# FFN weights split to fp16 halves in SBUF and turned by DMA, and an own attention order for block 0

## The chip, the cores and the metric

The kernel runs as one program on one core of one Trainium2 chip. The metric is the device time of one execution in microseconds. The engines of the core work side by side: TensorE (PE, the matrix engine, whose weight loads are shown apart as PEld), VectorE (DVE), ScalarE (ACT), GpSimd (POOL), and SyncE (SP), which here issues most of the DMA transfers. Each runs its own queue of instructions in order and waits for the others through semaphores. Data lie in HBM, in SBUF (128 partitions) and in PSUM (eight banks of 128 x 512 fp32 values), where matmuls write.

## The reference

There are 16 x 256 token ids below 128, so 4,096 positions that share 128 embedding rows. It computes, cut to what matters:

```
h = rms_norm(rms_norm(emb[x], norm_weight) @ proj.T)             # a table of 128 rows serves
q, k, v = layernorm(h) @ Wq.T, @ Wk.T, @ Wv.T                     # 16 heads of 32
q, k = layernorm(q * gamma + beta) / sqrt(32), layernorm(k * gamma + beta)
attn = where(tril, (q @ k.T) ** 2, 0)                             # per head, sequences of 256
h = h + (attn @ v / (attn.sum(-1) + eps)) @ Wo.T
x = fwht(layernorm(h) * SU_ug) / 64                               # Walsh-Hadamard over 512
a = silu(x @ W_gate.T * s_g) * (x @ W_up.T * s_u)                 # 2,048 wide
y = fwht(a * SU_dp) / 64                                          # Hadamard over 2,048
out = h + y @ W_down.T * s_d
```

## The kernel before

Every fp32 operand of a large product is kept as two fp16 halves, a high and a low (the low is what the high leaves of the value), and a product is three fp16 matmuls: high by high, high by low, low by high (`split_mm`, L1067 to L1069). The 4,096 positions are eight blocks of 512 (`NB`), two sequences each. Attention works on the table of 128 rows: `att` holds the squared scores of each pair of table rows, and for a block a matmul with one-hot ids picks columns of it (`picked`, L1204 and L1205), DVE multiplies them by causal counts (`prod<-bank,cnt`, L654, "product" below), ACT takes the high half and POOL the low half (L338) into `p16`. After four heads come the sums with `val` (`SUMS_AT`), the split of the head output `o16` (low half by POOL, L359), its flip on PE (eight 128x128 turns against a unit matrix, L1229, `O_FLIP_AT`) and ACT's copy to `oT`. Then, for each of four row tiles: output matmuls (`WO_AT`), a gathered table row added (`h_row<-h_table,ids_c`, L367, `ROWS_AT`), layer norm and the small Hadamard butterflies on DVE (L697 to L709, L428, L429), halves `x16` (L681), a flip (L1239) and a mix by a fp16 Hadamard matrix (L1247, L1248) into `xT`.

The program is made of slots, 32 to a block. In a slot the FFN of block b and the attention of block b+1 stand one behind the other on each engine (`feed(b, s)`, `attend(b + 1, s)`). Slots 0 to 15 hold one FFN tile each: gate half, up half (each 12 matmuls of 512 columns), ACT's silu gate `sg`, DVE's product `a<-bank,kap,sg` (L723), ACT's high half of `hid` and POOL's low half (L378). Slots 16 to 31 hold the down product, four row tiles, each finished on DVE (L731) and stored by SP (L287). Blocks 1 to 6 run in a loop. Block 0 stands apart: first the loads and the small matrices (table, Wq, Wk, Wv), then 32 slots of attention alone, then its FFN with attention of block 1 beside it.

The FFN's weights are made ready in block 0. Up and gate hold 32 units (128 columns by 512) and down 16. A unit of the first kind is turned on PE in fp32 against a diagonal of its row scales (`turn_unit`, L1062; the diagonals are made by DVE, `group_diag`, L451) into a PSUM bank; ACT copies the high half (L835, `unit`), DVE subtracts for the low (L457). Units 0 to 15 stand in the attention of block 0 (slots 2 to 17), the rest beside its FFN. The scales come from squares on ACT (`gu_square`), a power on POOL (`pair_power`, L316) and a rounding on DVE (`pair_scale`). A down unit is first mixed over rows by DVE (`down_mix`, two fp32 operations of 128x1024, L471 and L472), turned (`down_turn`), copied back by ACT, multiplied by the Hadamard matrix in fp32 (`down_hada`, L1110), and split from that bank by ACT (high) and DVE (low, L479). The order of everything is written out by hand: tuples of slot numbers and the order of the calls in each engine's section; there is no scheduler.

```
UNITS_IN_SLOT = (0, 0) + (1,) * BEFORE + (0,) * 14
DOWN_ORDER = (3, 2, 0, 1)
MIX_BESIDE = (1, 2, 3, 4, 5, 6, 7, 8, 9, 10, 11, 12, 12, 13)
SUMS_AT = (4, 8, 12, 15)
O_FLIP_AT = (5, 9, 13, 17)
ROWS_AT = (17, 19, 21, 23)
WO_AT = (18, 20, 22, 24)
X_FLIP_AT = (21, 23, 25, 27)
X_MIX_AT = (23, 25, 27, 29)
```

Of the kernel before, what the change touches and what calls it, by code (L numbers as in the profile page):

```python
# [52 lines left out]

def down_evicts(p):
    return [p - UNITS_BESIDE - 1] if UNITS_BESIDE < p <= UNITS_BESIDE + 16 else []


def units_beside(p):
    return [BEFORE + p] if p < UNITS_BESIDE else []


def tower(nc, x, emb, norm_w, proj_w, wq, wk, wv, wo, gamma, beta, su_ug, su_dp, wsc_ug, wsc_dp,
# [28 lines left out]
    with ctx:  # L91
# [9 lines left out]
        wgu = sb("wgu", [P, GROUPS, DC, 2, 512], F16)  # L101
# [15 lines left out]
        oT = sb("oT", [P, 2, QUADS, T], F16)  # L117
# [30 lines left out]
        k_o, k_d, s_w = gl[:, 0:1], gl[:, 1:2], gl[:, 10:12]  # L148

# [5 lines left out]
        GU = [words(wgu[:, n, :, :, :].rearrange("p a b c -> p (a b c)")) for n in range(GROUPS)]  # L155
# [47 lines left out]
        gu_ss gu_rn gu_pow gu_diag turned w_hi w_lo  # L203
        d_ss d_mix d_diag sc_ready bound_asked bound_sum bound_low bound_pow bound_done
        d_turned d_copied d_hada d_hi d_lo
# [7 lines left out]
        def column(n):  # L213

            return 4 * (n // 2) + FT * (n % 2)

# [9 lines left out]
        def _(sp):  # L226
# [4 lines left out]
            nc.sync.dma_start(late[:, 1536:1792], c_square).then_inc(S["c_land"], 16)  # L231
            nc.sync.dma_start(small_raw[0], quarters(proj_w)).then_inc(S["p_land"], 16)
            nc.sync.dma_start(nw_b, rows(norm_w, D)).then_inc(S["nw_land"], 16)
# [4 lines left out]
            def gu_load(n):  # L238
                w, g = (w_up if n % 2 else w_gate), n // 2
                for i in range(4):  # L240
                    rows_of_tile = w[512 * g + P * i:512 * g + P * i + P, :].rearrange("p (k d) -> p k d", k=DC)
                    nc.sync.dma_start(raw[n][:, :, i, :], rows_of_tile).then_inc(S[f"gu_land{n}"], 16)
# [12 lines left out]
            down_load(3)  # L255
            for n in range(2, GROUPS):
                gu_load(n)
            down_load(2)
# [5 lines left out]
            def load_ids_rows(n):  # L264
                sp.wait_ge(S["c_land"], 16)
                sp.wait_ge(S["onehotT_ready"], n)
                nc.sync.dma_start(ids_b[:, :], x_rows[bass.ds(n, 1), :].broadcast_to([P, T])).then_inc(S["ids_land"], 16)

            def load_ids_columns(n):
                sp.wait_ge(S["c_land"], 16)  # L270
                sp.wait_ge(S["hrow_land"], 64 * n)
                nc.sync.dma_start(ids_c[:, :], x_cols[bass.ds(n, 1), :, :].rearrange("a p c -> (a p) c"))\
                    .then_inc(S["idc_land"], 16)

            def block_io(b, n):

                for m in range(4):
                    if n is not None and m == 2:
                        load_ids_rows(n)
                    if n is not None and m == 3:  # L280
                        load_ids_columns(n)
# [3 lines left out]
                    else:  # L285
                        sp.wait_ge(S["y_last_done"], b + 1)
                    nc.sync.dma_start(out_rows[bass.ds(b, 1), m, :, :].rearrange("a p d -> (a p) d"), o_out[m][:, :])\  # L287
                        .then_inc(S["stored"], 16)
# [3 lines left out]
            with sp.Fori(0, NB - 2) as b:  # L292
                block_io(b, b + 2)
            block_io(NB - 2, None)
            block_io(NB - 1, None)
# [5 lines left out]
        def _(pool):  # L301
# [30 lines left out]
            pool.wait_ge(S["wo_scale"], 2)  # L332
            power(red[:, 3:4], red[:, 2:3]).then_inc(S["wo_scale"], 1)

            def product(n, h):
                if h < H:
                    pool.wait_ge(S["ph_done"], H * n + h + 1)
                    nc.gpsimd.tensor_tensor(p16[:, 1, h % 4, :], prod[:, h % 2, :], p16[:, 0, h % 4, :], ALU.subtract)\  # L338
                        .then_inc(S["pl_done"], 1)

            def first(n):
                return isinstance(n, int) and n == 0
# [11 lines left out]

            def attend(n, s):
                if s in SUMS_AT:
                    q = SUMS_AT.index(s)
# [3 lines left out]
                if s in ROWS_AT and not first(n):  # L361
# [3 lines left out]
                    pool.wait_ge(S["o_flipped"], QUADS * n + QUADS)  # L365
# [4 lines left out]
                if s in WO_AT:  # L370
                    m = WO_AT.index(s)
                    pool.wait_ge(S["ve_done"], 4 * n + m + 1)
                    power(rstd[:, m:m + 1], ve[:, m:m + 1]).then_inc(S["rstd_done"], 1)
# [7 lines left out]
            for s in range(SLOTS):  # L381
                product(0, s)
                attend(0, s)
                if s in NORM_AT:
# [12 lines left out]
            for s in range(SLOTS):  # L397
                feed(0, s)
                product(1, s)
                attend(1, s)  # L400
                if s == NORM_BESIDE:
                    pair_power(3)
# [12 lines left out]
        def _(dve):  # L415
# [22 lines left out]
            def pair_scale(g):  # L438
# [3 lines left out]
                link(nc.vector.tensor_scalar(pair_columns(rn, g), pair_columns(rnp, g), W_TOP, None, ALU.mult))  # L442

            def group_diag(n):
                c = slice(column(n), column(n) + 4)

                if n > 1:
                    dve.wait_ge(S["turned"], 4 * (n - 1))
                elif n == 1:
                    dve.wait_ge(S["t_ready"], 16)  # L450
                nc.vector.tensor_tensor(gu_diags[n], ident.rearrange("p (a b) -> p a b", a=1).broadcast_to([P, 4, P]),  # L451
# [955 lines left out]
```

## Time and profile before

| | us |
|---|---|
| median of 3 runs | 1418.95 (1417.93 to 1419.73) |
| the profiled execution | 1420.2 |
| its span in the profile | 1418.4 |
| before the first product of block 0 | 68.5 |
| block 0's heads, then its output rows | 59.9, then 38.4 |
| block 0's FFN beside block 1's attention | 211.5 |
| each middle block, six of them | 152.05 |
| last block's FFN | 127.8 |

The profile shows one execution. Times are us from the start of the span unless marked ns. In a row of a timeline the first number is the start and the second the duration; brackets at the end tell how long the engine was idle ahead of it and which engine's work ended that wait. In a row of a group, the numbers behind the bar are busy us in all, mean ns of one, and idle time ahead with its releasers. "Lnnn" is the line of the kernel. The ends of matmuls are modelled, so how fast they follow each other is read from their starts.

### The profile page before, as it was taken

To read this page: it belongs to the slowest core of one execution; us is meant where nothing else is said; L and a number is where in the kernel's file an instruction comes from. 1 tells how busy PE (TensorE), PEld (TensorE's weight loads), DVE (VectorE), ACT (ScalarE), POOL (GpSimd) and SP (SyncE) were. 2 spreads that over 40 slices of the span, in tenths; PEclk is the share of its full clock that TensorE was granted. 3 is DMA by queue.
4 is the path that set the end of the run, shared out by engine and by line. 5 is a ranking of instruction groups with operands and counts; after the bars stand their busy time and mean duration, and the time that the engine had idled before them with its cause. 6 is when DMAs were issued, how large, how long until landed. Compare 5 with 4: busy or idle time off the path is not lost.

```text
span 1418.4 us, 20319 instructions
## 1 busy us (share of the span) xinstructions
PE 1334.5 (94%) x7993; PEld 676.7 (48%) x7993; DVE 532.4 (38%) x1049; ACT 458.0 (32%) x767; POOL 423.6 (30%) x371
## 2 busy tenths in 40 slices
PE   5575598999999999999999999999999999999999
PEld 3363255554444444454454444544445444544444
DVE  1655567654322343226222432234223523251110
ACT  4453564441233223332243123412333224312220
POOL 0342143332143313432244213420434124420210
PEclk9887799999999999999999999999999999999999
DMA  8900000000100010001000100001000100010000
GB/s 288 287 14 1 1 0 1 1 0 31 38 1 1 23 39 8 0 9 45 16 1 1 45 24 0 1 31 38 1 1 9 51 9 1 1 46 15 0 1 30
DMA packets 34125, 39.42 MB, mean 28 GB/s; under 512 B 6596, under 2 KB 23288, under 8 KB 33528
## 3 DMA queue, kind: packets, MB, share of 16 engines
q1 hardware_dynamic: 30528, 28.99, 6.3%
q0 software_dynamic: 2560, 8.39, 2.0%
q8 instruction: 72, 1.18, 0.4%
q10 hardware_dynamic: 952, 0.75, 0.2%
q14 instruction: 13, 0.11, 0.0%
HBM read 29.47 MB, written 8.65 MB: 27 GB/s over the span
## 4 chain that ended last, share of the span: by engine, by line
PE 89%; DVE 5%; ACT 3%; issue 1%; POOL 1%; DMA 1%; SPq 0%; DVEq 0%; ACTq 0%
PE bank L1067 25%; PE bank L1068 25%; PE bank L1069 25%; PE bank L1219 3%; PE bank L1062 2%; PE bank L1204 2%; PE bank L1205 2%; PE bank L1229 1%; PE bank L1110 1%; PE bank L1239 1%; DMA hid<-in_L_tok_norm_weight 1%; PE bank L1060 1%; DVE wgu L457 1%; PE bank L1247 0%; PE bank L1248 0%
## 5 line engine op out<-in xcount | busy, mean ns | idle before, releaser
L1067 PE MATMUL bank<-xT,wgu 128*128 128x512 f16 x1024 | 389.0, 380 | 1.4 <-DVE xT L688 1.4
L1069 PE MATMUL bank<-xT,wgu 128*128 128x512 f16 x1024 | 389.1, 380 | 0.0
L1068 PE MATMUL bank<-xT,wgu 128*128 128x512 f16 x1024 | 389.1, 380 | 0.0
L378 POOL TENSOR_TENSOR hid<-a,hid 128x512 f16<-128x512 f32 x128 | 147.9, 1155 | 526.1 <-ACT hid L835 526.1
L723 DVE SCALAR_TENSOR_TENSOR a<-bank,kap,sg 128x512 f32<-128x512 f32 x128 | 96.1, 751 | 486.0 <-PE bank L1069 334.8
L1068 PE MATMUL bank<-wd,hid 128*128 128x512 f16 x512 | 194.0, 379 | 0.0
L1069 PE MATMUL bank<-wd,hid 128*128 128x512 f16 x512 | 194.0, 379 | 0.0
L1067 PE MATMUL bank<-wd,hid 128*128 128x512 f16 x512 | 194.0, 379 | 0.0
L338 POOL TENSOR_TENSOR p<-prod,p 128x512 f16<-128x512 f32 x128 | 153.2, 1199 | 135.8 <-ACT p L835 135.7
L835 ACT ACTIVATE hid<-a 128x512 f16<-128x512 f32 x128 | 80.6, 630 | 278.8 <-DVE a L723 278.8
L1069 PEld LDWEIGHTS bank<-xT,wgu 128*128 128x128 f16 x1024 | 100.3, 98 | 121.5 <-issue 1.1
L1067 PEld LDWEIGHTS bank<-xT,wgu 128*128 128x128 f16 x1024 | 100.4, 98 | 117.0 <-DVE xT L688 2.3
L1068 PEld LDWEIGHTS bank<-xT,wgu 128*128 128x128 f16 x1024 | 100.3, 98 | 114.3 <-issue 0.8
L982 ACT ACTIVATE sg<-bank,sc 128x512 f32<-128x512 f32 x128 | 87.2, 681 | 126.1 <-PE bank L1069 68.6
L835 ACT ACTIVATE p<-prod 128x512 f16<-128x512 f32 x128 | 79.7, 627 | 128.3 <-PE bank L1219 111.7
L835 ACT ACTIVATE sg<-wide,rstd 128x512 f16<-128x512 f32 x32 | 23.1, 722 | 219.7 <-DVE wide L429 219.7
L654 DVE TENSOR_TENSOR prod<-bank,cnt 128x512 f32<-128x512 f32 x128 | 86.6, 681 | 8.7 <-ACT cnt L835 8.0
L312 POOL TENSOR_TENSOR rstd<-ve,mhalf 128x1 f32<-128x1 f32 x32 | 32.3, 1009 | 188.5 <-DVE ve L706 188.5
L1069 PEld LDWEIGHTS bank<-wd,hid 128*128 128x128 f16 x512 | 50.1, 98 | 60.4
L1068 PEld LDWEIGHTS bank<-wd,hid 128*128 128x128 f16 x512 | 50.1, 98 | 58.3 <-issue 0.3
L1067 PEld LDWEIGHTS bank<-wd,hid 128*128 128x128 f16 x512 | 50.1, 98 | 58.1 <-issue 0.2
L697 DVE SCALAR_TENSOR_TENSOR h<-bank,gl,h_row 128x512 f32 (+1 forms) x28 | 21.0, 751 | 98.0 <-PE bank L1069 97.2
(183 smaller groups left out, 1389.5 us busy)
## 6 DMA issues: line engine op xcount, KB each, us to landing
out<-a SPq DMA_DIRECT2D x24, 256.0 KB, 2.1
wgu<-in_L_ffn_W_gate SPq DMA_DIRECT2D x16, 256.0 KB, 5.5
wgu<-in_L_ffn_W_up SPq DMA_DIRECT2D x16, 256.0 KB, 4.8
wd<-in_L_ffn_W_down SPq DMA_DIRECT2D x4, 1024.0 KB, 9.9
ids_b<-in_x SPq DMA_DIRECT2D x8, 256.0 KB, 4.2
out<-h_row SPq DMA_DIRECT2D x8, 256.0 KB, 2.0
xT<-in_L_tok_proj_weight SPq DMA_DIRECT2D x1, 1024.0 KB, 8.5
p<-in_L_attn_Wq SPq DMA_DIRECT2D x1, 1024.0 KB, 14.4
```

The costliest lines, as they stand in the source:

```text
L312: return nc.gpsimd.tensor_tensor(dst, src, mhalf[:, 0:src.shape[1]], ALU.pow)
L338: nc.gpsimd.tensor_tensor(p16[:, 1, h % 4, :], prod[:, h % 2, :], p16[:, 0, h % 4, :], ALU.subtract)\
L378: nc.gpsimd.tensor_tensor(hid[:, 1, s, :], a32[:, :], hid[:, 0, s, :], ALU.subtract)\
L654: nc.vector.tensor_tensor(prod[:, s % 2, :], PICK[s % 2][:, :], cnt[:, :], ALU.mult)\
L723: nc.vector.scalar_tensor_tensor(a32[:, :], bank[:, :], kap[:, s:s + 1], sg[:, :], ALU.mult, ALU.mult).then_inc(S["a_done"], 1)
L835: return nc.scalar.activation(dst, src, ACT.Copy, **kw)
L982: nc.scalar.activation(sg[:, :], bank[:, :], ACT.Silu, scale=sc[:, s:s + 1]).then_inc(S["silu_done"], 1)
L1062: last = mm(bank[:, i * P:(i + 1) * P], pieces(i), rights(i), start=True, stop=True)
L1067: mm(dst, w[0], v[0], start=first, stop=False)
L1068: mm(dst, w[0], v[1], start=False, stop=False)
L1069: return mm(dst, w[1], v[0], start=False, stop=final)
L1219: last = mm(HEADS[m // 2][:, 4 * (m % 2) + j, :], p16[:, p, j, m * P:(m + 1) * P], val[:, w, 4 * q + j, :], start=first, stop=final, skip_ ...
```

## The change

The change does five things.

1. The 32 gate and up units are no longer turned on PE. The raw rows lie in SBUF as loaded; the row scale multiplies them there, and a high and a low half go into `stage`, a ring of three buffers. For units 0 to 7 ACT scales and copies the high half and DVE subtracts the low (`unit_low`, L540); for units 8 to 31 POOL scales in place (`unit_scaled`, L422), ACT copies and POOL subtracts (`unit_low`, L426). SP then issues one DMA transpose for each unit from `stage` into `wgu` (`unit_turn`). Units 0 to 15 stand in slots 2 to 9 and 16 to 23 of block 0's attention, the rest two to a slot beside slots 0 to 7 of its FFN.
2. The 16 down units are mixed by DVE two to a slot in slots 0 to 7 of block 0's FFN, split three to a slot in slots 9 to 14, turned by DMA as well, and then multiplied by the Hadamard matrix as two fp16 matmuls, in the slot behind the split, in two banks by turns. ACT and DVE split the result as before.
3. In blocks 1 to 7 the flips of `o16` and `x16` are DMA transposes that SP issues (`o_turn`, `x_turn`), eight to a block. SP's loop over the blocks is written out. The row gather waits for the first output matmuls (`wo_ready`) instead of the last flip.
4. Block 0's attention keeps its flips on PE, and has an order of its own (the tables whose names end in 0), a second buffer for `p16`, and two banks for the gate in slots 0 to 7 of its FFN.
5. Ahead of it: `norm_w` is loaded before `proj_w`; each group of FFN weights is one load of 1 MB; the counts and small units 12 to 15 come earlier, and the value matmuls, the squares and split of Wo and its units go into the slots.

Of the tables of numbers and the changed functions, cut to the core:

```diff
+RING = 3
+UNIT_AT = tuple(range(2, 10)) + tuple(range(16, 24))
+UNITS_BESIDE = 8
+MIX_BESIDE = (0, 0, 1, 1, 2, 2, 3, 3, 4, 4, 5, 5, 6, 6, 7, 7)
+SPLIT_BESIDE = (9, 9, 9, 10, 10, 10, 11, 11, 11, 12, 12, 12, 13, 13, 13, 14)
...
+HEADS_AT0 = (4, 8, 12, 16)
+O_AT0 = (5, 9, 13, 16)
+O_FLIP_AT0 = (6, 10, 14, 17)
+WO_AT0 = (18, 19, 20, 21)
+X_HIGH_AT0 = (19, 20, 22, 23)
+X_FLIP_AT0 = (21, 22, 23, 24)
...
+        GATE0, UP0, D_HADA = [banks[0], banks[1]] * 4 + [banks[0]] * 8, banks[2], [banks[3], banks[1]]
...
+            def o_turn(n, q):
+                if q == 0:
+                    sp.wait_ge(S["wo_ready"], 4 * n)
+                sp.wait_ge(S["ol_done"], QUADS * n + q + 1)
+                nc.sync.dma_start_transpose(oT[:, q, :, :].rearrange("p l (m t) -> p (l m) t", t=P),
+                                            o16.rearrange("p l d -> p (l d)")).then_inc(S["oT_land"], 16)
+
+            def x_turn(n, m):
+                sp.wait_ge(S["xl_done"], 4 * n + m + 1)
+                sp.wait_ge(S["xhada_ready"], 4 * n + m)
+                nc.sync.dma_start_transpose(xn16.rearrange("p (k t) -> p k t", t=P),
+                                            x16.rearrange("p l d -> p (l d)")).then_inc(S["xn_land"], 16)
...
-                    pool.wait_ge(S["o_flipped"], QUADS * n + QUADS)
+                    pool.wait_ge(S["wo_ready"], 4 * n + 1)
...
+            def unit_scaled(x):
+                pool.wait_ge(S["gu_scaled"], x // 8 + 1)
+                nc.gpsimd.tensor_scalar(unit_raw(x), unit_raw(x), unit_scale(x), None, ALU.mult).then_inc(S["st_scaled"], 1)
+
+            def unit_low(x):
+                pool.wait_ge(S["st_hi"], x + 1)
+                nc.gpsimd.tensor_tensor(stage[x % RING][:, 1, :], unit_raw(x), stage[x % RING][:, 0, :], ALU.subtract)\
+                    .then_inc(S["st_low"], 1)
...
+            def unit_low(x):
+                dve.wait_ge(S["st_hi"], x + 1)
+                nc.vector.scalar_tensor_tensor(stage[x % RING][:, 1, :], unit_raw(x), unit_scale(x), stage[x % RING][:, 0, :],
+                                               ALU.mult, ALU.subtract).then_inc(S["st_lo"], 1)
...
+            def down_hada(v):
+                if v > 1:
+                    pe.wait_ge(S["d_lo"], v - 1)
                 if v == 0:
...
+                pe.wait_ge(*landed(UNITS + v))
+                w = wd[:, DOWN_ORDER[v // 4], v % 4, :, :, :].rearrange("p l f d -> p l (f d)")
+                mm(D_HADA[v % 2][:, :], hada16[:, :], w[:, 0, :], start=True, stop=False)
+                mm(D_HADA[v % 2][:, :], hada16[:, :], w[:, 1, :], start=False, stop=True).then_inc(S["d_hada"], 1)
```

How the order moves at three places. First POOL, in slots 0 to 3 of block 0's FFN. Before (`hid<-a,hid` is the FFN tile's low half, `p<-prod,p` the low half of a head, `h<-h,mhalf` a power for the scales):

```order
L378 TENSOR_TENSOR hid<-a,hid 128x512
L338 TENSOR_TENSOR p<-prod,p 128x512
L378 TENSOR_TENSOR hid<-a,hid 128x512
L338 TENSOR_TENSOR p<-prod,p 128x512
L378 TENSOR_TENSOR hid<-a,hid 128x512
L338 TENSOR_TENSOR p<-prod,p 128x512
L316 TENSOR_TENSOR h<-h,mhalf 128x2x4
L378 TENSOR_TENSOR hid<-a,hid 128x512
```

And after, in slots 1 and 2 (`wgu<-wgu,h` scales a unit in place, `h<-wgu,h` is its low half):

```order
L422 TENSOR_SCALAR wgu<-wgu,h 128x512 x2
L461 TENSOR_TENSOR hid<-a,hid 128x512
L426 TENSOR_TENSOR h<-wgu,h 128x512 x2
L433 TENSOR_TENSOR p<-prod,p 128x512
L422 TENSOR_SCALAR wgu<-wgu,h 128x512 x2
L461 TENSOR_TENSOR hid<-a,hid 128x512
```

Two operations to a slot have become six: the scalings stand ahead of the tile's low half, the low halves of the units ahead of the head's.

Second DVE, in slot 10 (and the first row of slot 11) of block 0's FFN. Before (`wd<-wd` mixes, `wd<-bank3,gl,wd` is the low half of a finished down unit):

```order
L654 TENSOR_TENSOR prod<-bank4,cnt 128x512
L479 SCALAR_TENSOR_TENSOR wd<-bank3,gl,wd 128x512
L723 SCALAR_TENSOR_TENSOR a32<-bank1,kap,sg 128x512
L479 SCALAR_TENSOR_TENSOR wd<-bank3,gl,wd 128x512
L471 TENSOR_TENSOR wd<-wd 128x1024
L472 SCALAR_TENSOR_TENSOR wd<-wd 128x1024
L654 TENSOR_TENSOR prod<-bank5,cnt 128x512
```

And after (`h1<-wd,wsd_s,h1` is the low half of a down unit ahead of its turn, in `stage`):

```order
L735 TENSOR_TENSOR prod<-bank4,cnt 128x512
L834 SCALAR_TENSOR_TENSOR a32<-bank2,kap,sg 128x512
L540 SCALAR_TENSOR_TENSOR h1<-wd,wsd_s,h1 128x512 x3
L558 SCALAR_TENSOR_TENSOR wd<-bank3,gl,wd 128x512
L558 SCALAR_TENSOR_TENSOR wd<-bank1,gl,wd 128x512
L558 SCALAR_TENSOR_TENSOR wd<-bank3,gl,wd 128x512
L735 TENSOR_TENSOR prod<-bank5,cnt 128x512
```

The three low halves of the next units stand ahead of the three that finish the last ones; the mixes are gone from here.

Third SP, for one middle block. Before (a store of a row tile each, and the next ids):

```order
L287 DMA out<-a 128x512
L284 REGISTER_ALU
L287 ISA
L287 DMA out<-a 128x512
L266 REGISTER_ALU
L267 ISA
L267 DMA ids_b<-in_x 128x512
L284 REGISTER_ALU
L287 ISA
L287 DMA out<-a 128x512
L271 REGISTER_ALU
L272 DMA ids_c<-in_x 128x4x1
```

And after:

```order
L327 DMA_TRANSPOSE oT<-h_row 128x8x128 x4
L333 DMA_TRANSPOSE prod<-sg 128x8x128
L352 DMA out<-a 128x512
L333 DMA_TRANSPOSE prod<-sg 128x8x128
L352 DMA out<-a 128x512
L333 DMA_TRANSPOSE prod<-sg 128x8x128
L306 DMA ids_b<-in_x 128x512
L352 DMA out<-a 128x512
L333 DMA_TRANSPOSE prod<-sg 128x8x128
L311 DMA ids_c<-in_x 128x4x1
L352 DMA out<-h_row 128x512
```

The four turns of `o16` (its place in SBUF is named `h_row` here) stand ahead of the block's stores, and the four of `x16` (`prod<-sg`) between them, the fourth behind the third store.

## Rows read from the trace of the kernel before

**Rows 1.** The page, busy time of each engine in us, share, instructions.

```profile
PE 1334.5 (94%) x7993; PEld 676.7 (48%) x7993; DVE 532.4 (38%) x1049; ACT 458.0 (32%) x767; POOL 423.6 (30%) x371
```

**Rows 2.** Windows: length, busy us (instructions) by PE, PEld, DVE, ACT, POOL; PEclk, DMA share, GB/s.

```profile
68.50:128.40 59.90, 36.84 (x381) 30.70 (x381) 31.61 (x74) 32.48 (x63) 26.50 (x23) 0.80 0.06 16
128.40:166.80 38.40, 20.30 (x91) 8.94 (x91) 23.72 (x57) 17.40 (x39) 6.25 (x6) 0.72 0.00 1
166.80:378.30 211.50, 201.79 (x1216) 112.64 (x1217) 123.22 (x200) 85.67 (x154) 61.42 (x47) 0.98 0.03 11
530.40:682.40 152.00, 152.00 (x925) 73.62 (x924) 51.83 (x106) 45.14 (x69) 49.41 (x44) 1.00 0.05 17
```

**Rows 3.** Timeline of PE in a middle block: start, duration, line, operation.

```profile
1087.98 0.61 PE L1229 MATMUL bank<-c,h_row 128*128 128x128 f16 x8
1088.43 0.38 PE L1067 MATMUL bank<-wd,hid 128*128 128x512 f16 x1
1088.64 0.38 PE L1068 MATMUL bank<-wd,hid 128*128 128x512 f16 x1
...
1091.02 0.38 PE L1067 MATMUL bank<-wo_t,oT 128*128 128x512 f16 x1
```

**Rows 4.** Groups of instructions in block 0's FFN, 166.8 to 378.3.

```profile
L378 POOL TENSOR_TENSOR hid<-a,hid 128x512 f16<-128x512 f32 x16 | 18.5, 1157 | 99.8 <-ACT hid L835 99.8
...
L1062 PE MATMUL bank<-h,wgu 128*128 128x128 f32 x128 | 17.9, 284 | 2.5 <-DVE wgu L457 1.7 <-DVE h L451 0.7
L1062 PE MATMUL bank<-h,wd 128*128 128x128 f32 x128 | 17.8, 285 | 1.8 <-DVE h L528 1.8
...
L1110 PE MATMUL bank<-h 128*128 128x512 f32 x32 | 17.4, 626 | 2.1 <-DVE wd L479 2.1
```

**Rows 5.** Timeline of DVE and POOL in block 0's FFN.

```profile
187.05 1.22 DVE L471 TENSOR_TENSOR wd<-wd 128x1024 f32<-128x1024 f32 x1
187.07 2.21 POOL L338 TENSOR_TENSOR p<-prod,p 128x512 f16<-128x512 f32 x1
...
188.30 2.07 DVE L472 SCALAR_TENSOR_TENSOR wd<-wd 128x1024 f32<-128x1024 f32 x1
...
205.45 1.23 DVE L472 SCALAR_TENSOR_TENSOR wd<-wd 128x1024 f32<-128x1024 f32 x1
```

**Rows 6.** Timeline ahead of and in block 0's heads, PE and DVE.

```profile
54.03 3.70 PE L1177 MATMUL bank<-oT,hid 128*128 128x512 f32 x8 [0.69 <-ACT oT L835]
...
56.88 0.16 DVE L615 TENSOR_REDUCE h<-h 128x1 f32<-128x4 f32 x1 [9.33 <-ACT sg L832]
...
76.04 0.69 DVE L654 TENSOR_TENSOR prod<-bank,cnt 128x512 f32<-128x512 f32 x1 [0.68 <-PE bank L1205]
...
85.67 0.69 DVE L654 TENSOR_TENSOR prod<-bank,cnt 128x512 f32<-128x512 f32 x1
...
88.14 0.68 DVE L654 TENSOR_TENSOR prod<-bank,cnt 128x512 f32<-128x512 f32 x1
```

**Rows 7.** Timeline of DVE and PE in block 0's FFN: tile products 0 and 8, first down matmul.

```profile
176.01 0.75 DVE L723 SCALAR_TENSOR_TENSOR a<-bank,kap,sg 128x512 f32<-128x512 f32 x1 [0.65 <-PE bank L1069]
...
245.03 0.75 DVE L723 SCALAR_TENSOR_TENSOR a<-bank,kap,sg 128x512 f32<-128x512 f32 x1 [0.91 <-issue]
...
322.57 0.38 PE L1067 MATMUL bank<-wd,hid 128*128 128x512 f16 x1
```

**Rows 8.** Timeline of POOL, ACT and DVE in the same middle block.

```profile
1085.05 1.15 POOL L359 TENSOR_TENSOR h_row<-wide,h_row 128x512 f16<-128x512 f32 x1 [0.56 <-ACT h_row L835]
...
1128.95 0.59 ACT L835 ACTIVATE xT<-bank 128x512 f16<-128x512 f32 x1
...
1130.18 0.74 DVE L731 SCALAR_TENSOR_TENSOR a<-bank,gl,h 128x512 f32<-128x512 f32 x1
```

**Rows 9.** DMA issues: tiles, queue, kind, count, KB each, median us to landing.

```profile
out<-a SPq DMA_DIRECT2D x24, 256.0 KB, 2.1
...
wgu<-in_L_ffn_W_up SPq DMA_DIRECT2D x16, 256.0 KB, 4.8
```

More of the change, by code:

```diff
@@ L331, in _ @@
             pair_power(0)
[L332 to L342, printed above, removed]
             def first_rows():
@@ L919, in product @@
             def product(n, s):
-                if s == 0:
+                if s == 0 and not first(n):
                     act.wait_ge(S["count_ready"], n + 1)
@@ L926, in product @@
                     act.wait_ge(S["p_done"], i + 1)
-                    if s % 4 == 0:
+                    if s % 4 == 0 and not first(n):
                         act.wait_ge(S["heads_ready"], QUADS * n + s // 4)
-                    copy(p16[:, 0, s % 4, :], prod[:, s % 2, :]).then_inc(S["ph_done"], 1)
+                    if s % 4 == 0 and s >= 8 and first(n):
+                        act.wait_ge(S["heads_ready"], s // 4 - 1)
+                    copy(p_pair(n, s)[:, 0, s % 4, :], prod[:, s % 2, :]).then_inc(S["ph_done"], 1)
@@ new lines, in head_high, with xT_high @@
+            def head_high(n, q):
+                act.wait_ge(S["o_done"], QUADS * n + q + 1)
+                if not first(n) and not (isinstance(n, int) and q == 0):
+                    act.wait_ge(S["oT_land"], 16 * (QUADS * (n - 1) + q))
+                copy(o16[:, 0, :], wide[:, :]).then_inc(S["oh_done"], 1)
+            def xT_high(n, m):
+                act.wait_ge(S["xhada_ready"], 4 * n + m + 1)
+                if m == 0:
+                    act.wait_ge(S["up_ready"], FT * n)
+                copy(xT[:, 0, :, m * P:(m + 1) * P], PICK[1][:, :].rearrange("p (k t) -> p k t", t=P))\
+                    .then_inc(S["xThi_done"], 1)
@@ L931, in attend, with x_high @@
+            def x_high(n, m):
+                act.wait_ge(S["xm_done"], 4 * n + m + 1)
+                act.wait_ge(S["rstd_done"], 4 * n + m + 1)
+                if first(n):
+                    act.wait_ge(S["flip_ready"], m)
+                elif not (isinstance(n, int) and m == 0):
+                    act.wait_ge(S["xn_land"], 16 * (4 * (n - 1) + m))
+                copy(x16[:, 0, :], wide[:, :], scale=rstd[:, m:m + 1]).then_inc(S["xh_done"], 1)
             def attend(n, s):
+                if s - 1 in WO_AT:
+                    x_high(n, WO_AT.index(s - 1))
@@ L1155, in _, with count @@
                 last.then_inc(S["qk_ready"], 1)
+            def count(n, bank):
+                for i in range(2):
+                    c = SEQ * i
+                    mm(bank[:, c:c + SEQ], onehot[:, 2 * i, :], cum0, start=True, stop=False)
+                    last = mm(bank[:, c + P:c + SEQ], onehot[:, 2 * i + 1, :], cum1, start=False, stop=True)
+                last.then_inc(S["count_ready"], 1)
+            pe.wait_ge(S["par_land"], PARAMS)
+            pe.wait_ge(S["onehot_ready"], 2)
+            count(0, COUNT0)
+            pe.wait_ge(S["wv_diag"], 2)
+            for u in range(12, 16):
+                small_unit(u)
             def qk_turn(i):
@@ L1263, in feed_half @@
             def feed_half(s, half, bank, done):
-                n = 2 * (s // 4) + half
-                c = slice(P * (s % 4), P * (s % 4) + P)
+                n, i = 2 * (s // 4) + half, s % 4
                 for k in range(DC):
-                    last = split_mm(bank[:, :], [wgu[:, n, k, l, c] for l in range(2)],
+                    last = split_mm(bank[:, :], [wgu[:, n, i, l, k, :] for l in range(2)],
                                     [xT[:, l, k, :] for l in range(2)], k == 0, k == DC - 1)
@@ L1357, in _ @@
                 attend(1, s)
+                for v in down_third(s, 2):
+                    down_hada(v)
             pe.wait_ge(S["y_done"], 3)
```

747 lines of the change are left out of this document (377 added, 370 removed).

## The prediction

> **What bounds the kernel now.** The page first: TensorE (PE) is busy 94% of the span, the other engines under 40% [rows 1]. So I cut the span where PE changes its work and read the windows [rows 2]. A middle block is PE solid for 152.0 us: 512-column fp16 matmuls start every 0.216 us (1088.43, 1088.64), and a flip of eight turns holds the queue from 1087.98 to 1088.43, 0.45 us [rows 3]. Ahead of block 0's FFN it is otherwise: in the heads (68.5 to 128.4) and the output rows (128.4 to 166.8) PE is busy 57 of 98 us, and a chain over DVE, ACT and POOL sets the pace. Block 0's FFN takes 211.5 us, 59.5 more than a middle block, and holds the fp32 turns and Hadamards: 17.9, 17.8 and 17.4 us in three groups [rows 4]. Those sums count the overlap of neighbouring matmuls, so I take 53 less a fifth, 43 us, for what they hold of the queue.
>
> **The port.** [rows 5] decides much of what follows. POOL's subtraction took 2.21 us at 187.07 where its kind takes 1.16 [rows 4]; beside it ran VectorE's (DVE's) fp32 mix from 187.05 (1.22), and the next mix took 2.07 where an undisturbed one took 1.23 (205.45). The three fit if POOL waits for the first mix and the second mix for POOL: a POOL operation and a DVE operation with two SBUF inputs take turns. The Trainium skill (GPSIMD Engine Reference, the table of SBUF interfaces at its head) says that GpSimd shares SBUF ports with DVE and contends with DVE instructions of two SBUF inputs. By that rule, which this trace bears out, the change is costlier than a count of busy time tells: the old splits read PSUM and SBUF, the new ones read SBUF twice.
>
> **The change, part by part.**
>
> *Before the heads.* DVE waited 9.33 us for the squares behind which Wo's stood, until 56.88 [rows 6]. Those squares, Wv's diagonals and small units 12 to 15 now stand elsewhere, so head 0's product follows the features: they end at 47.6; two turns, a copy and the scores 3.1; a square, two highs and a low 2.5; a pick 0.4. That is 53.6. The norm weight is issued one transfer earlier; I give that 1.5 us, by choice between nothing and the 4.8 of a 256 KB piece [rows 9]. Product 0 at 52 for 68.5. Behind it two picks 0.9, the value matmuls 3.7 (54.03), pick 2 0.4 and handovers 0.8: product 2 at 57.8 where it was at 76.04 [rows 6]: -18.2.
> *Heads.* An old slot with a unit, product to product, took 2.47 us (85.67 to 88.14). A new one: product 0.64, ACT copy 0.6; then ACT's high 0.6 and DVE's low, which reads two SBUF tensors when POOL's product (1.16) has begun: 0.64 + 0.6 + 1.16 + 0.7 = 3.1. Eight slots 25; fit and two head rows 4; slots 10 to 15, without units, 12.5; then POOL's queue ahead of the last heads (pair 1's power, two scalings, two products, the last low, flip and copy) 12.7. That is 54.2 for 52.4 (76.0 to 128.4): +1.8.
> *Output rows.* The new order overlaps the low half of row m-1 with row m; alone I take 36 for 38.4. But POOL now has a scaling and a subtraction in each slot, 2 us beside the five two-input operations of a row's norm, and ACT a split and a square: +2 for each of four rows. 44.2: +5.8. The FFN starts at 156.2, -10.6 in all.
> *Block 0's FFN, slots 0 to 7.* PE needs 24 x 0.216 + 0.43 = 5.6 us a slot. POOL: two scalings, feed, two lows, product = 4 x 1.16 + 2c. The price c of a one-input POOL operation has no row; 1.16 above, half of it below; I take 0.9. DVE: two mixes, four operations of 1.23, all of two inputs, so they take turns with POOL: 6.4 + 4.9 + 1.1, while POOL waits for ACT's split and copy, = 12.4. The next product needs POOL's feed of the last, and PE's next up half needs the product. The first product comes at 9.2 (176.01 - 166.8); three slots go at some 10.2 while the queues fill, four at 12.4, and the slot without units at 9.5: product 8 ends at 99, before at 78.2 (245.03 - 166.8) [rows 7].
> *Slots 9 to 15.* Product 9 at 104. Hadamard 0 stands ahead of the next up half and needs the first turn: split 1.3, low 0.7, turn T + 0.1; with T = 3.3, 5.4 later. From slot 10 on, third 2's Hadamard waits on PE for the low half of third 0 (two banks), and on DVE that low half stands behind three new splits, which wait for ACT. From the end of an up half: product 0.85, ACT copy 0.6, high 0.6, first split 0.6, then DVE 3 x 0.65 and the low half 0.65 = 5.2; PE had work for 0.9. A slot is 5.2 + 0.43 + 2.6 + 0.43 + 2.6 = 11.3, four times, the fifth 9.9, then 5.6 + 0.7. The first down matmul comes 170.8 after the FFN's start; before, 322.57 - 166.8 = 155.8 [rows 7]: +15. PE's own work fell by 43 - 6.9, but is not what ends here.
> *Turns by DMA, blocks 1 to 7.* PE loses eight flips, 3.58 us a block, and ACT eight copies of 1.0. Were PE bound throughout, that is the gain. POOL ends the last low half at 1086.20 [rows 8]; Wo, at 1091.02 [rows 3], would come 0.45 earlier, so T may be 4.4. The row gather waits for Wo instead of the flip, which brings row 0 3.4 us later, but it catches up 1.1 a row. The fourth x turn stands on SP behind the third store: from the mix of slot 27, 0.2 + ACT 0.6 + DVE 0.7 + finish 0.75 [rows 8] + issue 0.45 = 2.7; the mix of slot 29 is 24 x 0.216 = 5.2 away. So T may be 2.5 there. T has no row: a store of the same 256 KB lands in 2.1 us, a weight piece in a full queue in 4.8 [rows 9]. I take 3.3, with a store in front; bounds 2.1 and 4.8. Stall 0.8, so -2.8 a block: six blocks -16.7, block 0's second half -2.2 + 0.8 = -1.4. Were T 2.1, seven blocks gain 5.6 more; at 4.8, 7 x 1.9 + 1.5 = 15 less.
> The Trainium skill has two prices. Advanced Engine Details and Errata, X-Bar Transpose, calls such DMAs as fast as regular ones, which fits the range; VectorE: DVE Perf Modes, The three transpose paths, has 1309 ns for one 128x128 by DMA and 390 ns on TensorE. Eight blocks in a row by that table would be an estimate of 10.5 us and the time over 1500; no run here shows either.
>
> **Sum** against the profiled execution: -10.6 + 15 - 1.4 - 16.7 = -13.7; 1420.2 - 13.7 = 1406.5. The median of the three runs is 1.25 lower, so 1405.
>
> **Rivals.**
> A: POOL and DVE do not hold each other. Slots 0 to 7 then follow POOL alone, 6.4 + 1.1 = 7.5 to 8: product 8 at 67, -32; heads -5, rows -6: 1362. For it: one pair of kinds is all that [rows 5] shows. 0.17.
> B: the three-unit slots do not stall, because ACT and DVE run ahead of PE: -20: 1385. The order of the queues speaks against it. 0.07.
> C, slower: turns land late. From T = 3.3 every us costs 7 (fourth x turn) and 1 (Hadamard 0), above 4.4 another 7 (Wo). 8 x 1.1 = 8.8, then 4.9 / 15 = 0.3: from T = 4.7 on the kernel is slower. At 6 it is 8.8 + 24 + 4 (slots 10 to 13) more: 1442. For it: a turn is 2-byte pieces, and the 256 KB weight piece took 4.8 already; against: SP's queue is empty in these stretches, and 2.1 is what it then takes. 0.22.
> D, no change: the later gather holds the rows 2 us more a block: 7 x 2 = 14, 1419. 0.08, half of it slower.
> My own case, 0.46: 1380 to 1428, by c (0.6 to 1.16: -4, +3), T (-6, +15) and chains of 5 us each way in four stages; of it 0.41 faster, 0.03 same, 0.02 slower.
>
> **Numbers.** No change is within 0.2% (2.8 us), about what a measurement can tell. Faster 0.41 + 0.17 + 0.07 = 0.65, same 0.03 + 0.04 = 0.07, slower 0.02 + 0.22 + 0.04 = 0.28. Leaving out half of C and the last of A, 8 in 10 lie in 1365 to 1440.
>
> **What would show it.** Wo's first matmul near 112, the FFN's first near 156; DVE's a<-bank in slots 3 to 7 some 12 us apart, with mixes and POOL rows above 2 us; in slots 10 to 13 PE waiting for DVE's wd of two units back, 11 us a slot; first down matmul at 327; middle blocks of 149.3, with one gap of 0.8 us at the last matmul that reads prod. It is wrong if the turn DMAs land in over 4.7 us, if mixes stay at 1.23 beside POOL, or if middle blocks take 148.5 or more than 151.

## The result, and the profile after

The changed kernel took 1425.76 us (median of 4 runs, 1425.33 to 1427.61); the kernel before, run again beside it, 1418.44 (1415.86 to 1419.73). The ratio is 1.0056, with a 95% interval of 1.0039 to 1.0074: slower by 7.3 us where I forecast 14 faster. The two profiled executions, which everything below compares, lie 5.1 us apart.

The page of the changed kernel, busy time and PE's granted clock in 40 slices, beside [rows 1]:

```profile
span 1423.5 us, 18640 instructions
...
PE 1280.5 (90%) x7161; PEld 599.2 (42%) x7161; DVE 540.8 (38%) x1030; ACT 406.7 (29%) x711; POOL 497.4 (35%) x419
...
PEclk9656788888999999999999999999999999999999
```

PE was busy 54 us less and the span grew by 5.1. The windows by stage, which answer to [rows 2] (columns as there): the heads until the output rows' first matmul, the output rows, block 0's FFN to tile product 9, from there to its first down matmul, and a middle block:

```profile
52.00:115.40 63.40, 30.73 (x281) 16.90 (x282) 35.49 (x72) 34.24 (x69) 34.30 (x29) 0.61 0.31 73
115.40:156.00 40.60, 20.54 (x91) 8.65 (x92) 24.85 (x50) 17.21 (x35) 22.63 (x18) 0.71 0.28 52
156.00:258.60 102.60, 70.39 (x366) 31.04 (x367) 78.33 (x99) 41.33 (x86) 85.47 (x55) 0.84 0.25 47
258.60:341.80 83.20, 54.88 (x284) 23.13 (x283) 32.52 (x50) 32.24 (x53) 18.43 (x15) 0.85 0.29 54
546.86:696.50 149.64, 149.02 (x861) 69.71 (x860) 51.72 (x106) 37.72 (x61) 49.30 (x44) 1.00 0.13 31
```

| stage | before | forecast | after |
|---|---|---|---|
| head 0's product at | 68.5 | 52 | 52.0 |
| FFN of block 0 starts at | 166.8 | 156.2 | 156.0 |
| from there to product 8 | 78.2 | 99 | 91.2 |
| to product 9 | 88.6 | 104 | 102.7 |
| to the first down matmul | 155.8 | 170.8 | 185.8 |
| first down matmul to next block | 55.7 | 54.3 | 55.4 |
| six middle blocks | 912.3 | 895.6 | 898.5 |
| last FFN | 127.8 | 127.8 | 127.8 |

By stage: -10.8, +30.0, -0.3 and -13.8, together the 5.1 of the spans. Three stages came within 3 us of their terms. One did not: between product 9 and the first down matmul lie 83.2 us, before 67.2, forecast 66.8. Slot 11 of it, from its tile product to the gate half of slot 12, changed kernel, timeline of PE and DVE:

```profile
283.20 0.75 DVE L834 SCALAR_TENSOR_TENSOR a<-bank,kap,sg 128x512 f32<-128x512 f32 x1 [4.68 <-issue]
...
285.83 2.08 DVE L540 SCALAR_TENSOR_TENSOR h<-wd,wsd_s,h 128x512 f16<-128x512 f32 x3 [1.88 <-ACT h L942]
...
287.83 1.40 DVE L558 SCALAR_TENSOR_TENSOR wd<-bank,gl,wd 128x512 f16<-128x512 f32 x2
288.63 0.56 PE L1201 MATMUL bank<-wd,hada 128*128 128x512 f16 x1 [4.66 <-DVE wd L558]
...
289.83 0.64 PE L1186 MATMUL bank<-xT,wgu 128*128 128x512 f16 x1
290.26 0.63 PE L1187 MATMUL bank<-xT,wgu 128*128 128x512 f16 x1
...
292.27 0.38 PE L1186 MATMUL bank<-xT,wgu 128*128 128x512 f16 x1
292.49 0.38 PE L1187 MATMUL bank<-xT,wgu 128*128 128x512 f16 x1
```

The third Hadamard waits 4.66 us for the low half that stands behind three others (L540 x3): the stall as forecast. What I had left out follows it: the matmuls then start 0.43 us apart for three microseconds, the lower of the clock's two levels (1.2 GHz), before they return to 0.22 (2.4 GHz). Between 262 and 340, 56 matmuls start late, most of them 0.43 us behind the last: 10.8 us in all.

The slow matmuls aren't settled by the wait alone. The run "Norm weight late" below has the same code in slots 9 to 15. Slot 14 there and in the changed kernel, first the changed kernel, timeline of PE:

```profile
327.58 0.61 PE L1201 MATMUL bank<-wd,hada 128*128 128x512 f16 x1 [3.33 <-DVE wd L558]
327.98 0.63 PE L1202 MATMUL bank<-wd,hada 128*128 128x512 f16 x1
```

```profile
330.38 0.39 PE L1201 MATMUL bank<-wd,hada 128*128 128x512 f16 x1 [3.33 <-DVE wd L558]
330.61 0.38 PE L1202 MATMUL bank<-wd,hada 128*128 128x512 f16 x1
```

The wait is 3.33 us in both. In the first, 13 matmuls behind it are slow and the slot takes 13.1 us (granted clock 0.74), in the second none is and it takes 10.4 us (1.00). So 2.7 of the 83.2 us were the luck of this execution; in the other the stage took 80.5.

### The profile page after: what moved, and what is told of

The parts are those of the page before. It is cut to its first block and busy times, and to the rows that moved or that the text cites. A ratio compares the mean times of both kernels' runs of the same rounds, so it can differ in the third digit from the quotient of the medians.

```text
span 1423.5 us, 18640 instructions
## 1 busy us (share of the span) xinstructions
PE 1280.5 (90%) x7161; PEld 599.2 (42%) x7161; DVE 540.8 (38%) x1030; ACT 406.7 (29%) x711; POOL 497.4 (35%) x419
## 5 line engine op out<-in xcount | busy, mean ns | idle before, releaser
L1185 PE MATMUL bank<-xT,wgu 128*128 128x512 f16 x1024 | 396.5, 387 | 5.5 <-DVE a L834 4.0
L1186 PE MATMUL bank<-xT,wgu 128*128 128x512 f16 x1024 | 395.7, 386 | 0.0
L1187 PE MATMUL bank<-xT,wgu 128*128 128x512 f16 x1024 | 394.8, 386 | 0.0
L461 POOL TENSOR_TENSOR hid<-a,hid 128x512 f16<-128x512 f32 x128 | 149.7, 1170 | 479.2 <-ACT hid L942 479.2
L433 POOL TENSOR_TENSOR p<-prod,p 128x512 f16<-128x512 f32 x120 | 141.4, 1181 | 121.1 <-ACT p L942 121.1
L1185 PEld LDWEIGHTS bank<-xT,wgu 128*128 128x128 f16 x1024 | 102.1, 100 | 131.4 <-issue 10.5
L1187 PEld LDWEIGHTS bank<-xT,wgu 128*128 128x128 f16 x1024 | 101.7, 99 | 126.0 <-issue 9.1
L942 ACT ACTIVATE hid<-a 128x512 f16<-128x512 f32 x128 | 80.5, 629 | 255.1 <-DVE a L834 255.1
L1186 PEld LDWEIGHTS bank<-xT,wgu 128*128 128x128 f16 x1024 | 101.7, 99 | 122.0 <-issue 8.1
L942 ACT ACTIVATE p<-prod 128x512 f16<-128x512 f32 x120 | 74.2, 624 | 118.9 <-PE bank L1326 107.3
L735 DVE TENSOR_TENSOR prod<-bank,cnt 128x512 f32<-128x512 f32 x128 | 86.5, 680 | 11.4 <-ACT cnt L942 9.4
```

The lines of the kernel that those rows point to most:

```text
L433: nc.gpsimd.tensor_tensor(pair_of_head[:, 1, h % 4, :], prod[:, h % 2, :], pair_of_head[:, 0, h % 4, :], ALU.subtract)\
L461: nc.gpsimd.tensor_tensor(hid[:, 1, s, :], a32[:, :], hid[:, 0, s, :], ALU.subtract)\
L735: nc.vector.tensor_tensor(prod[:, s % 2, :], PICK[s % 2][:, :], cnt[:, :], ALU.mult)\
L942: return nc.scalar.activation(dst, src, ACT.Copy, **kw)
L1185: mm(dst, w[0], v[0], start=first, stop=False)
L1186: mm(dst, w[0], v[1], start=False, stop=False)
```

## The experiments

Where a row says "product 9", it is the tile product's start behind the FFN's start. A time without a number of runs is of one run; the four of the changed kernel lie within 2.3 us, and differences of that size are read from the stages alone.

**Low half first.** DVE's queue in slots 10 to 14:

```
-                feed(0, s, UP0)
+                for v in down_third(s, 0):
+                    down_unit(v)
+                feed(0, s, UP0)
...
-                for v in down_third(s, 0) + down_third(s, 1):
+                for v in down_third(s, 1):
```

> The changed kernel, with DVE's low half of the first finished down unit of a slot put ahead of the tile product, so that the third Hadamard (same bank) need not wait for three new low halves. Theory 1, order of DVE's queue plus slow matmuls behind each wait: slots 10 to 14 took 13.4 us each; with the wait of 4.66 us gone a slot is PE's 6.9 us, or, since the first Hadamard of the next slot then waits for its turn (about 3.2 us after its issue), some 10 to 11 us. Five slots: 12 to 17 us off, time 1409 to 1414. Rival, the latency of the turns sets these slots already: no change, 1424 to 1427. Either way slots 0 to 8 stay as they were (product 8 at 91 us after the FFN's start).

1416.51 us: 9 off, less than the theory's 12 to 17. From product 9 to the first down matmul it took 71.3 us for 83.2. The wait for DVE went, and the one for the turn came (timeline of PE, this kernel):

```profile
278.54 0.38 PE L1203 MATMUL bank<-wd,hada 128*128 128x512 f16 x1 [2.95 <-DMA wd<-h]
...
288.57 0.59 PE L1203 MATMUL bank<-wd,hada 128*128 128x512 f16 x1 [2.96 <-DMA wd<-h]
...
311.48 0.49 PE L1203 MATMUL bank<-wd,hada 128*128 128x512 f16 x1 [2.91 <-DMA wd<-h]
```

Slots took 9.9 to 13.0 us for 13.4. The first and second of these waits are alike, but behind the first no matmul is slow (a slot of 10.0 us) and behind the second 15 are (13.0). Both mechanisms are there, one behind the other: an order that frees DVE's low half uncovers the turn's latency.

**No mixes.** The butterflies of the down weights cut to one column, so the down weights stay unmixed:

```
-                link(nc.vector.tensor_tensor(v[:, :, 1, :], v[:, :, 0, :], v[:, :, 1, :], ALU.subtract))
+                link(nc.vector.tensor_tensor(v[:, :, 1, 0:1], v[:, :, 0, 0:1], v[:, :, 1, 0:1], ALU.subtract))
```

> The changed kernel with DVE's mixes of the down weights cut to a sliver of one column of each piece (the down weights are left unmixed, so this work is left out). Theory 1, POOL and DVE take turns at SBUF: with four DVE operations of two SBUF inputs gone from each of slots 0 to 7, POOL's operations fall back to 1.15 and 1.56 us, a slot to POOL's 7.8 plus about 1 us, and product 8 stands at 75 to 80 us after the FFN's start for 91.2: 11 to 16 us off, time 1410 to 1415. Rival, POOL's own work sets these slots whatever DVE does: product 8 at 88 to 91, time 1423 to 1426. Second rival, DVE's own queue sets them: product 8 below 70, since PE needs only 5.6 us a slot.

1409.28 us, product 8 at 74.6: the theory's case, a little better. POOL's operations in this kernel, and what the same kinds took in the changed one (timeline of POOL, then of POOL and DVE in the changed kernel):

```profile
195.91 1.15 POOL L433 TENSOR_TENSOR p<-prod,p 128x512 f16<-128x512 f32 x1
197.03 3.10 POOL L422 TENSOR_SCALAR wgu<-wgu,h 128x512 f32<-128x512 f32 x2
```

```profile
165.89 4.32 POOL L426 TENSOR_TENSOR h<-wgu,h 128x512 f16<-128x512 f32 x2
...
167.12 2.07 DVE L551 SCALAR_TENSOR_TENSOR wd<-wd 128x1024 f32<-128x1024 f32 x1
169.22 2.06 DVE L550 TENSOR_TENSOR wd<-wd 128x1024 f32<-128x1024 f32 x1
...
170.17 2.13 POOL L433 TENSOR_TENSOR p<-prod,p 128x512 f16<-128x512 f32 x1
```

Beside mixes a subtraction takes 2.1 us and a mix 2.07; apart they take 1.15 and 1.22. It is the pattern of [rows 5]: they take turns. In this kernel all of POOL's low halves in slots 0 to 8 are back at about 1.15 us, and its scalings at 1.56. Its work in a slot is 3.10 + 1.16 + 2.27 + 1.15 = 7.7 us, and a slot took 8.3 in the mean, so it is the likely bound. This run also takes DVE's own 4.9 us of mixes out of each slot, so it does not show how much of the 16.6 us is the port and how much DVE's queue.

**Flips only.** The kernel before with this part of the change alone: `o_turn` and `x_turn` on SP in blocks 1 to 7, its loop written out, PE's flips kept for block 0 (`if first(n) and s in O_FLIP_AT`), the gather behind `wo_ready`. In part:

```
-                    pool.wait_ge(S["o_flipped"], QUADS * n + QUADS)
+                    pool.wait_ge(S["wo_ready"], 4 * n + 1)
...
+            for q in range(QUADS):
+                o_turn(1, q)
+            for b in range(NB):
+                block_io(b)
```

> The kernel before, with one part of the change alone: the flips of the head outputs and rows of blocks 1 to 7 as DMA transposes, and the row gather behind the first output matmuls. Theory 1, this part is worth what the middle blocks of the changed kernel show: six blocks from 152.05 to 149.7 us, and 0.3 to 1.5 us in block 0's FFN: 1403 to 1405. Rival, the gain of the middle blocks needs something else of the change (the split gate banks, a shorter block 0): middle blocks stay above 151 and the time above 1412.

1403.83 us (4 runs, 1402.96 to 1405.31), ratio 0.9903 (0.9881 to 0.9924). This part alone makes the kernel 1% faster. A middle block of it:

```profile
538.00:688.00 150.00, 149.32 (x864) 70.01 (x862) 51.74 (x106) 37.73 (x61) 49.66 (x45) 1.00 0.14 31
```

The six took 900.1 for 912.3, near the 898.5 of the changed kernel. Its profiled execution also began its FFN at 163.5 instead of 166.8, with nothing changed ahead of it but the layout of `oT`: the loads landed earlier (the norm weight was used at 11.71 for 13.04). So some 3 us of the changed kernel's -10.8 are likely the profiled execution of before, not the change. The kernels below that share the changed kernel's code up to there have product 0 at 51.6 to 53.4, so one profile tells such a start only to a microsecond or two.

**ACT and DVE split units 16 to 31.** POOL's `unit_scaled` and `unit_low` are gone beside the FFN; ACT copies with the scale, DVE subtracts:

```
-                for x in units_beside(s):
-                    unit_scaled(x)
                 feed(0, s)
-                for x in units_beside(s):
-                    unit_low(x)
```

> The changed kernel, with units 16 to 31 split as units 0 to 7 are: ACT scales and takes the high half, DVE the low half, and POOL has no part in it (four POOL operations of a slot, 2 x 1.56 + 2 x 1.15 us, replaced by two DVE operations of about 1.1 us and ACT scaling as it copies). Theory 1: DVE is then the busiest, 0.65 + 0.75 + 4 x 1.23 + 2 x 1.13 = 8.6 us a slot and up to 1 us of collisions: product 8 at 75 to 80 us after the FFN's start, time 1410 to 1415. Rival, DVE was the bound already and gets two operations more: product 8 at 95 to 105, time 1430 to 1440.

1416.88 us, 9 off; product 8 at 86.2, between the theory (75 to 80) and the changed kernel's 91.2, product 9 at 92.4 for 102.7. The window to product 9 shows what took over:

```profile
156.20:248.60 92.40, 74.50 (x377) 32.42 (x378) 84.55 (x116) 42.87 (x86) 36.54 (x23) 0.86 0.28 49
```

DVE is busy 84.6 of 92.4 us, and PE waits for its tile product (1.28 and 2.36 us behind products 3 and 4; the matmuls behind the first keep their spacing of 0.22, behind the second they fall to 0.43 after four). My 8.6 us a slot allowed up to 1 us of collisions; slots took 9.2 and more, and 9 of the 32 mixes still took 2.06 us or more.

**Hadamards half a slot later.** The first behind the up half, the second behind the attention, the third behind the next slot's gate half, on PE, ACT and DVE alike. PE's part:

```
                     feed_half(s, 0, GATE0[s], S["gate_ready"])
-                    for v in down_third(s, 0):
+                    for v in down_third(s - 1, 2):
                         down_hada(v)
...
                     feed_half(s, 1, UP0, S["up_ready"])
-                    for v in down_third(s, 1):
+                    for v in down_third(s, 0):
                         down_hada(v)
```

> The changed kernel with the three down Hadamards of a slot moved later by half a slot on PE, ACT and DVE: the first behind the up half, the second behind the attention, the third behind the gate half of the next slot. Each turn then has 5 us and more to land, and each bank a half slot to be emptied. Theory (now in two parts: the wait for DVE's low half with one order, the wait for the turn with the other, and after each wait some 8 matmuls at double spacing): both waits go, slots 10 to 14 take 7 to 8 us for 13.4, and the first down matmul comes 50 to 58 us after product 9 for 83.2: time 1395 to 1402. Rival: DVE and ACT cannot do three splits and three evictions in such a slot (5.9 and 6.1 us by their rows, beside 1.4 and 1.9 of the attention's): slots above 9 us, time above 1405.

1399.05 us, 27 off, by order alone. From product 9 to the first down matmul it took 54.4 us for 83.2, in the range. The window of that stage:

```profile
259.60:314.00 54.40, 44.47 (x285) 19.83 (x284) 32.57 (x50) 31.91 (x53) 18.35 (x15) 1.00 0.48 83
```

The work is that of the fourth window above (285 matmuls, 32.6 us of DVE), the granted clock 1.00 for 0.85. The waits for the low half are shorter, not gone: none is over 2.1 us, where they were 3.3 to 4.7. Slots 10 to 13 took 8.7 to 9.8, more than the 7 to 8 expected; the rival was right that DVE and ACT now set them (PE waits for the low half, and DVE 1.88 us a slot for ACT's high half), and wrong on the time.

**Both.** The last two edits together.

> Both edits together: units 16 to 31 split by ACT and DVE without POOL, and the down Hadamards half a slot later. Theory: the two stages add up; product 9 at 92 us after the FFN's start as without the second edit, then 50 to 58 us: time 1384 to 1392. Rival: the gain of one is lost in the other because both queue on DVE: above 1395.

1388.50 us: 1425.8 - 8.9 - 26.7 = 1390.2 if they only added. They do, within what single runs tell.

**Mixes spread,** on top of both:

```
-MIX_BESIDE = (0, 0, 1, 1, 2, 2, 3, 3, 4, 4, 5, 5, 6, 6, 7, 7)
+MIX_BESIDE = (0, 0, 1, 2, 2, 3, 4, 4, 5, 6, 6, 7, 8, 9, 10, 11)
```

> As the run with both edits, and the mixes spread over slots 0 to 11 (one or two to a slot) instead of two in each of slots 0 to 7. In slots 0 to 7 PE waited 1.3 to 2.4 us a slot for DVE's tile product, which stood behind two mixes. Theory, DVE's queue is the bound of these slots: product 9 comes at 78 to 84 us for 92, slots 9 to 11 grow by at most 1 us each: 6 to 12 us faster than the run with both edits. Rival, something else paces them (the single up bank, ACT): less than 3 us.

1388.14 us: a miss. Product 9 came at 85.7 for 91.6, but product 9 to the first down matmul took 60.2 for 55.2. The mixes moved into slots 8 to 11 lengthened that stage by 5.0 us where the other gained 5.9: DVE's work was moved, and by this it bounds both stages.

**Fourth turn ahead of the third store.**

```
                     if b + 2 < NB and m == 2:
                         load_ids_rows(b + 2)
+                    if b + 1 < NB and m == 2:
+                        x_turn(b + 1, 3)
```

> The changed kernel with the fourth turn of x16 issued by SP ahead of the block's third store instead of behind it. Theory: PE's one gap of 0.87 us in a middle block, at the last mix, is this turn standing behind the store; it shrinks to the spacing of 0.22, so the six middle blocks take 149.0 to 149.2 us each for 149.75, and the time falls by 3 to 5 us to 1421 to 1423. Rival: the turn is late for its latency alone, and the gap stays.

1421.72 us, 4.0 off, as expected. The gap of the changed kernel, and SP's queue there:

```profile
687.25 0.34 SPq L352 DMA_DIRECT2D out<-a  x1
687.68 1.30 SPq L333 DMA_TRANSPOSE prod<-sg  x1
...
690.83 0.39 PE L1357 MATMUL bank<-prod,hada 128*128 128x512 f16 x1 [0.49 <-DMA prod<-sg]
```

In the edited kernel the turn is issued at 684.60 and PE has no idle row there; middle blocks take 148.9 to 149.7, 895.05 for six, 3.4 less.

**All that helped**, the spread mixes, and the second sum over the bound (where PE had stood 5.64 us in slot 2) one slot later on all engines. PE's part of that:

```
-                    if s == BOUND_BESIDE + 1:
+                    if s == BOUND_BESIDE + 2:
                         bound_sum(1)
```

> The edits that helped, together: units 16 to 31 split by ACT and DVE, down Hadamards half a slot later, mixes spread over slots 0 to 11, the fourth turn of x16 ahead of the third store; and one new edit, the second sum over the bound moved one slot later on all engines, because PE stood 5.64 us there (waiting for DVE's terms in slot 2). Theory: 1388.1 less 3.4 for the turn and 3 to 5 for the sum: 1379 to 1382. Rival: the wait in slot 2 returns as a wait for DVE's tile product, which is behind the same mixes: 1383 to 1386.

1380.69 us (4 runs, 1378.55 to 1381.77), ratio to the kernel before 0.9733 (0.9712 to 0.9754): it beats both kernels, and lies in the theory's range. The rival is there too: PE's waits for the tile product grew from 7.6 us in the run before to 11.2. The windows to product 9 and on to the first down matmul:

```profile
157.30:240.90 83.60, 71.17 (x378) 31.45 (x378) 76.03 (x111) 42.95 (x86) 37.70 (x23) 0.90 0.33 57
240.90:300.30 59.40, 45.14 (x271) 19.48 (x272) 40.17 (x57) 31.68 (x53) 18.47 (x15) 0.94 0.44 76
```

DVE is the busiest engine that is left: 76 of 83.6 us.

**Norm weight late.** The changed kernel with the two loads in their old order.

> The changed kernel with the norm weight loaded behind the projection weight, as before the change. In the changed kernel the table's first scaling started at 9.86 us and waited for nothing of this load; before, it started at 13.04. Theory: the whole chain to head 0's product follows it, so product 0 moves from 52.0 to 54.5 or 55.5 and the time grows by 2.5 to 3.5 us. Rival, the term I gave it (1.5 us, because Wq's landing comes next): product 0 at 53.5.

1427.66 us, which is no more than the slowest run of the changed kernel (1427.61), so the time shows nothing. In the profile DVE's first scaling waited for this load until 11.77 (9.86 in the changed kernel), product 0 came at 54.2, 2.3 later, and the FFN 2.7 later. That is between theory and rival, and the load itself landed sooner than in the profile of before (13.04). The first down matmul came at 341.9, as in the changed kernel (341.8): slot 14 gave the 2.7 us back by its clock.

```profile
11.77 0.75 DVE L631 SCALAR_TENSOR_TENSOR hid<-hid,cnt 128x512 f32<-128x512 f32 x1 [2.06 <-DMA hid<-in_L_tok_norm_weight]
```

## Why the prediction was wrong

*The time* lay in the range, the sign was wrong. The sum was off by 18.8 us on the spans (-13.7 forecast, +5.1 measured), of which 15.0 lie in one term, "+15" for block 0's FFN up to the first down matmul.

*Slots 9 to 15* failed: the stall was right and its price was not, above all because the sum had no term for slow matmuls. By pieces:

| piece | forecast | measured | of it slow matmuls | the rest |
|---|---|---|---|---|
| product 9 at | 104 | 102.65 | | -1.4 |
| product 9 to 10 | 5.4 | 11.33 | 1.5 | 4.4 |
| four slots | 45.2 | 53.5 | 6.6 | 1.7 |
| the fifth | 9.9 | 13.1 | 2.7 | 0.5 |
| the last | 6.3 | 5.2 | 0 | -1.1 |

The first is a slip. The 5.4 us are the time at which Hadamard 0 can start, and the sum went on from there as if product 10 stood there too. Behind it come its own two matmuls and an up half, 3.3 us as measured, and it started 1.2 us later than forecast. The second is the clock: "A slot is 5.2 + 0.43 + 2.6 + 0.43 + 2.6 = 11.3" took every half slot at full speed. It measured 13.4, of which 1.5 to 1.7 us are slow matmuls and 0.4 to 0.5 a longer chain over ACT and DVE (the wait was 4.66 us for 5.2 - 0.9 = 4.3). The fifth slot's wait was in its 9.9; the slow matmuls behind it were not, and another execution had none there (10.4). Slow matmuls are 10.8 of the 15.0 us. The runs show the rest: with the order changed no wait for a low half or a turn is over 2.1 us, the clock reads 1.00 and the stage takes 54.4. A clock below full speed was visible before the change, in [rows 2] (0.72 and 0.80 in stages where PE waits), and I put no price on it.

*The cause of the stall* was right: the third Hadamard behind DVE's three low halves. So rival B (no stall) fell. The forecast did not see that the turn's latency lay close behind it, as the run with the low half first showed.

*Slots 0 to 8*: that product 9 came within 1.4 us of its 104 is luck, for two errors cancel. Product 8 came at 91.2 for 99, and from there to product 9 it took 11.4 us for 5. The second part, changed kernel, timeline of POOL and PE:

```profile
247.01 2.27 POOL L426 TENSOR_TENSOR h<-wgu,h 128x512 f16<-128x512 f32 x2
249.23 1.15 POOL L433 TENSOR_TENSOR p<-prod,p 128x512 f16<-128x512 f32 x1
250.44 1.56 PE L1326 MATMUL bank<-val,p 128*128 128x33 f16 x48 [9.50 <-POOL p L433]
```

PE's sums of slot 8 need the head's low half, which on POOL stands behind the last two units' low halves. Product 8 is at 247.19, so PE stood some 3 us (the 9.50 is too long, because the trace lacks matmuls ahead of it). The gate and up half of slot 9 come only after the sums, and their first matmuls are slow.

For the first part, the port was right (POOL's rows above 2 us, 14 of the 32 mixes at 1.96 to 2.07), but adding up the times of both engines was not: the other mixes ran in 1.2 to 1.6. Against it, c was 1.56 us, above my upper bound of 1.16. With this c my sum would give 13.8 us for each of slots 3 to 6; they took 11.0 in the mean. This scaling has one tensor input, a scale per partition and an fp32 output, the subtraction of 1.15 us has two inputs and an fp16 output; no run shows which of these makes it dearer. Rival A fell; taking POOL's part away (ACT and DVE instead) gave 5 us to product 8, taking the mixes away gave 16.6.

*Heads and output rows*: -18.2 was -17.3; +1.8 was +4.3, with c in it; +5.8 (36 + 4 x 2 is 44.0, so +5.6) was +2.2. Near in sum, with some 3 us of it due to late loads in the profile of before.

*Turns by DMA*: T was 3.1 to 3.2 for 3.3. The forecast gap was 0.8; PE started its last mix 0.65 late. That it was the place on SP's queue was shown by moving it. Without the gap a middle block still took 149.2, so the flips were worth 2.9 us a block and not 3.58. Rivals C (late turns) and D (late gather) did not happen in the blocks 1 to 7. The Trainium skill gives 1309 ns for one 128x128 turned by DMA (VectorE: DVE Perf Modes, The three transpose paths); eight times that, my estimate of 10.5 us, is not borne out for eight blocks in one transfer. The Trainium skill also calls such transfers as fast as regular ones (Advanced Engine Details and Errata, X-Bar Transpose); this trace nearly agrees, with 3.1 us beside 2.2 for a store of 256 KB. DMA issues of the changed kernel, median us to landing at the end:

```profile
out<-a SPq DMA_DIRECT2D x24, 256.0 KB, 2.2
...
oT<-h_row SPq DMA_TRANSPOSE x28, 3.1
...
prod<-sg SPq DMA_TRANSPOSE x28, 3.1
...
wd<-h SPq DMA_TRANSPOSE x16, 3.2
```

## What to carry to other kernels

Price a stall of TensorE twice: the wait, and the matmuls behind it that run at the lower clock. In the changed kernel the six waits of 3.3 to 4.7 us each cost 1.5 to 2.7 us more; in other executions waits of about 3 us cost from nothing to 2.9 us, so this term is a range and not a number. When weights begin to arrive by DMA, look at which engine empties the PSUM bank they are multiplied into and what stands ahead of that on its queue, and give each transfer half a slot more: that order was worth 27 us, more than the whole change was meant to bring. A change of many parts can hide a good one: the flips alone gave 1%. Check a sum piece by piece: a total that fits at one point (product 9) can hold two errors of 6 us and more.

## What the hardware did that I had not expected

POOL's fp32 scaling of 128x512 with a scale per partition took 1.56 us, its subtraction of two tensors with fp16 output 1.15. A DMA transpose held SP's queue for 1.23 us, a store for 0.34. Behind the same wait of 3.33 us at the same place, PE ran at 0.43 us a matmul in one execution and at 0.22 in another. Even a tiny operation of DVE can be held by POOL: one of 128x2 took 1.07 us and ended with the POOL operation beside it, its neighbour took 0.17 (timeline of DVE and POOL in the changed kernel):

```profile
254.00 0.17 DVE L598 RECIPROCAL gl<-gl 128x2 f32<-128x2 f32 x1
254.09 1.15 POOL L442 TENSOR_TENSOR h_row<-wide,h_row 128x512 f16<-128x512 f32 x1
254.20 1.07 DVE L599 TENSOR_SCALAR gl<-gl 128x2 f32<-128x2 f32 x1
```
